# Gated cross-attention and expert layer on one core: the last four second groups of a block are issued between the first groups of the next block

## The reference

```
x = x + tanh(g_xattn) * attention(layernorm(x), ctx, ctx, mask)
t = layernorm(x)                                   # [4096, 128]
gate = softmax(t @ Wg + bg)                        # 8 experts
thr  = sigmoid(t @ Wt + bt) * 0.125
w = max(gate - thr, 0);  w = w / sum(w)
h  = gelu(einsum('td,edf->etf', t, W1) + b1)       # 8 experts x 512
eo = einsum('etf,efd->etd', h, W2) + b2
out = x + tanh(g_ffn) * einsum('te,etd->td', w, eo)
```

## Time and profile before

| what | value |
|---|---|
| median of 3 runs | 737.56 us (735.87 to 740.76) |
| profiled execution, its own time | 733.51 us |
| its span (first to last instruction) | 731.4 us |
| mean granted TensorE clock | 0.975 of full |
| busy: TensorE, VectorE, ScalarE, GpSimd | 89%, 71%, 58%, 25% of the span |

### The profile page before, as it was taken

How to read it: one execution, slowest core, us unless ns; L and a number is a source line. 1 busy time by engine, 2 the same in 40 slices (tenths; PEclk the granted TensorE clock), 3 DMA queues, 4 the chain that set the end, 5 groups by cost and what they waited for, 6 DMA issues and landing times.

```text
span 731.4 us, 14293 instructions
## 1 busy us (share of the span) xinstructions
PE 647.9 (89%) x3944; PEld 482.2 (66%) x3944; DVE 522.8 (71%) x1083; ACT 422.0 (58%) x764; POOL 179.7 (25%) x218
## 2 busy tenths in 40 slices
PE   3679888888899888884799999999999999999996
PEld 2446566556666666542587787877878778787784
DVE  5577676677677766662578687786877868778786
ACT  4225555555555555543575776757766676676673
POOL 6133333322333222321012022121221212202122
PEclk9879999999999999998799999999999999999999
DMA  6333333333333333330311112111111111211120
GB/s 189 109 97 104 103 98 97 91 83 104 94 99 96 92 95 104 103 97 2 49 60 45 57 44 59 53 49 56 44 57 43 57 44 56 57 43 50 40 67 14
DMA packets 48420, 53.09 MB, mean 73 GB/s; under 512 B 9616, under 2 KB 34832, under 8 KB 48400
## 3 DMA queue, kind: packets, MB, share of 16 engines
q1 hardware_dynamic: 48400, 52.85, 26.3%
HBM read 27.01 MB, written 2.23 MB: 40 GB/s over the span
## 4 chain that ended last, share of the span: by engine, by line
PE 65%; DVE 9%; issue 7%; DMA 6%; ACT 5%; SPq 4%; POOL 3%; DVEq 1%; POOLq 0%; ACTq 0%
PE ps_y L1067 8%; PE ps_y L1069 7%; PE ps_y L1068 7%; PE ps_h L1089 7%; PE ps_h L1087 7%; PE ps_h L1088 7%; PE scores L1025 5%; DMA k_masked<-k_stack 5%; PE scores L1026 4%; SPq L396 4%; POOL yT L544 3%; ACT part L577 2%; DVE k_stack L702 2%; PE scores L1017 2%; PE misc L886 2%
## 5 line engine op out<-in xcount | busy, mean ns | idle before, releaser
L650 ACT ACTIVATE h_sb<-ps_h,b_sb 128x512 f32<-128x512 f32 x256 | 175.2, 689 | 116.5 <-PE ps_h L1089 103.2
L857 DVE TENSOR_TENSOR h_low<-h_sb,h_high 128x512 fp32r<-128x512 f32 x256 | 164.5, 683 | 0.0
L544 POOL TENSOR_TENSOR yT<-yT,weighted 128x512 f32<-128x512 f32 x56 | 72.3, 1290 | 309.2 <-DVE weighted L845 308.5
L853 DVE CAST h_high<-h_sb 128x512 fp32r<-128x512 f32 x128 | 87.0, 680 | 81.6 <-ACT h_sb L650 81.6
L679 DVE TENSOR_REDUCE neg_max<-scores 128x4 f32<-128x512 f32 x128 | 86.7, 689 | 70.8 <-PE scores L1026 70.1
L563 ACT ACTIVATE probs<-scores 128x512 f32<-128x512 f32 x128 | 77.1, 604 | 60.0 <-PE scores L1018 60.0
L1067 PE MATMUL ps_y<-h_high,w_high 128*128 128x512 f32 x256 | 102.2, 399 | 5.0 <-DVE h_low L857 5.0
L1087 PE MATMUL ps_h<-x_high,w_high 128*128 (+1 forms) x256 | 101.8, 398 | 0.0
L1069 PE MATMUL ps_y<-h_high,w_low 128*128 128x512 f32 x256 | 101.3, 396 | 0.0
L1089 PE MATMUL ps_h<-x_high,w_low 128*128 (+1 forms) x256 | 101.0, 394 | 0.0
L1068 PE MATMUL ps_y<-h_low,w_high 128*128 128x512 f32 x256 | 100.8, 394 | 0.0
(11 more groups left out here) (122 smaller groups left out, 981.5 us busy)
## 6 DMA issues: line engine op xcount, KB each, us to landing
w_row<-w_scratch SPq DMA_DIRECT2D x64, 256.0 KB, 3.2
k_masked<-k_stack SPq DMA_DIRECT2D x64, 128.0 KB, 2.5
k_cur<-k_stack SPq DMA_DIRECT2D x16, 512.0 KB, 3.0
q_masked<-q_stack SPq DMA_DIRECT2D x64, 96.0 KB
w_raw<-in_w_ffn SPq DMA_DIRECT2D x17, 256.0 KB, 2.7
ctx_sb<-in_ctx SPq DMA_DIRECT2D x17, 128.0 KB, 2.1
out_y<-y_out SPq DMA_DIRECT2D x8, 256.0 KB, 3.4
mask_words<-in_mask SPq DMA_DIRECT2D x17, 32.0 KB, 1.8
```

Of the source, the lines that this page charges most:

```text
L544: nc.gpsimd.tensor_tensor(yT[:], yT[:], weighted[:, e % 2, :], ALU.add).then_inc(added, 1)
L650: nc.scalar.activation(h_sb[:, j % HBUF, :], ps_h[:, j % 4, :], ACT.Gelu_apprx_tanh, bias=b1_sb[:, j:j + 1]).then_inc(h_done, 1)
L853: V.tensor_copy(h_high[:, j % HBUF, :], h_sb[:, j % HBUF, :]).then_inc(high_odd, 1)
L857: V.tensor_tensor(h_low[:, j % HBUF, :], h_sb[:, j % HBUF, :], h_high[:, j % HBUF, :].bitcast(F32), ALU.subtract).then_inc(low2_done, 1)
```

## The change

TensorE: in blocks 1 to 7, s(28) to s(31) of the block before are issued behind h(0) to h(3), in the places where the LAG leaves a gap. Those of the last block follow the loop. The output transposes of the block before move from behind h(2) to behind s(2), which is behind h(6) (j == LAG + 2). s(0) now waits for combine 6 of the block before, no longer for combine 7 (the wait on weighted_done is g * E + (e - 1) for all e).

VectorE: combines 6 and 7 of the block before move to steps 0 and 4 of the next block, behind low(j + 1), and finish(g - 1) from step 2 to step 6. Those of the last block follow the loop.

GpSimd, ScalarE and SyncE have unchanged programs.

```diff
--- before.py
+++ after.py
@@ -861,13 +861,16 @@
                     high(j + 1)
                     low(j)
                     low(j + 1)
-                    if j == 2 and not (isinstance(g, int) and g == 0):
+                    later = not (isinstance(g, int) and g == 0)
+                    if j % FC == 0 and j >= FC + LAG:
+                        combine(g, (j - LAG) // FC - 1)
+                    elif j % FC == 0 and later:
+                        combine(g - 1, (j + CH - LAG) // FC - 1)
+                    if j == LAG + 2 and later:
                         finish(g - 1)
-                    if j >= FC + LAG and j % FC == 0:
-                        combine(g, (j - LAG) // FC - 1)
-                for e in range((CH - LAG) // FC - 1, E):
-                    combine(g, e)
             loop_b(dve, body_b)
+            combine(NB - 1, E - 2)
+            combine(NB - 1, E - 1)
             finish(NB - 1)
 
 
@@ -1059,7 +1062,7 @@
                 e, f = divmod(j, FC)
                 if f == 0:
 
-                    wait_count(pe, weighted_done, g * E + (e - 1) if e >= 2 else g * E)
+                    wait_count(pe, weighted_done, g * E + (e - 1))
                 pe.wait_ge(high_odd if j % 2 else high_even, g * (CH // 2) + (j // 2 + 1))
                 pe.wait_ge(low2_done, g * CH + (j + 1))
                 dst = ps_y[:, e % 2, :]
@@ -1087,13 +1090,16 @@
                     mm(dst, w_high[:, e, cols], xh, start=True, stop=False)
                     mm(dst, w_high[:, e, cols], xl, start=False, stop=False)
                     mm(dst, w_low[:, e, cols], xh, start=False, stop=True).then_inc(h_full, 1)
-                    if j == 2 and not (isinstance(g, int) and g == 0):
-                        untranspose(g - 1)
+                    later = not (isinstance(g, int) and g == 0)
                     if j >= LAG:
                         second(g, j - LAG)
-                for j in range(CH - LAG, CH):
-                    second(g, j)
+                    elif later:
+                        second(g - 1, CH + j - LAG)
+                    if j == LAG + 2 and later:
+                        untranspose(g - 1)
             loop_b(pe, body_b)
+            for j in range(CH - LAG, CH):
+                second(NB - 1, j)
             untranspose(NB - 1)
```

## The result

The changed kernel takes 755.64 us (median; 754.03 to 756.41) against 736.71 before on the same chip: ratio 1.0244, 95% interval 1.0200 to 1.0287. It is **slower**, by 18.9 us. Forecast were 751.2 and a range of 744.3 to 757.5. One execution of e1_t_late, 880.03 us at a mean granted clock of 0.68, was in a slow state and counts in no ratio.

A forecast was written before the change was run, and what follows sets the result against it. TensorE was taken as the bound, with 1.99 us lost at each of seven block seams. Seams +10.9 and clock falls +2.7 on 737.56 gave 751.2 us, range 744.3 to 757.5.

The forecast's parts named there:

- The wait of s(30) goes: At block seams, s(30), a second matmul group, no longer waits for VectorE's h_low; saves 0.68 us and a 0.1 hitch.
- h(0) waits instead, 0.36: At a block's first matmul group, TensorE waits for the gelu of group 31 of the block before; 0.36 us with hitch.
- T waits 2.69: A block's four output transposes, behind s(2), wait 2.69 us for the last add, which follows VectorE's moved combine 7.
- VectorE and GpSimd have room: At seams, the copy beside add 6 adds 0.76 us to VectorE, covered by 0.8 at least; finish costs nothing.
- Transfers hidden: Output store and w_row loads are not delayed; expert 3's load has 16 groups of 1.38 us against 3.2 landing time.
- Seam +1.56: Each of seven block seams costs 3.55 us after against 1.99 before: +1.56, seven times +10.9 us.
- rival D: VectorE falls behind at seams: copy beside add 6 and finish add 0.8 us each, 756.8 us; 5%.
- The clock: TensorE's 2.5 us idle at T lowers the clock in one to two of seven seams, 1.8 us each: +2.7 us.
- Rival A: Every seam loses the clock: +23.5 us, 761.1 us; 5%.
- B: At seams T does not wait, the last add being over when TensorE gets there: 729.7 us, faster; 5%.

The follow-up runs named there:

- e1_t_late: Changed kernel with the output transposes T two slots later (behind s(4), not s(2)) and finish in step 10: 729.06 us, 0.9931 of before.
- e5_h0_wait: Changed kernel with h(0) to h(3) waiting for the gelu of the group four back, not all 32 groups of the block before: 746.17 us, 1.0147 of before.
- e9_filler_h0: Changed kernel with 11 unused matmuls ahead of T's wait and h(0) to h(3) waiting only for the group four back: 745.77 us, 1.0130 of before.
- e4_t_plus1: Changed kernel with T one slot later (behind s(3)) and finish in step 8: 739.45 us, 1.0058 of before.
- e2_combine_early: Changed kernel with only combine 7 moved, from step 4 to step 2 on VectorE; T stays behind s(2): 735.21 us, 0.9997 of before.
- e3_filler: Changed kernel with 11 extra unused matmuls ahead of T's wait in blocks 1 to 7: 749.94 us, 1.0190 of before.

## Why the prediction was right

By its steps:

1. *The wait of s(30) goes.* It did; one h_low wait is left at each end of the stage.
2. *h(0) waits instead, 0.36.* Right in place and cause, and it comes in all seven seams, though the waits list six: in the first seam h(0) is only 0.24 late. The term was too small for the others: 0.44 and a hitch of 0.1, 0.54 (e5_h0_wait and e9_filler_h0: 3.8 to 3.9 us in seven). The hop from ScalarE to TensorE was taken as 0.06 to 0.13 and is 546.19 - 545.95 = 0.24 in this seam.
3. *T waits 2.69.* 2.54 in the first seam, 2.70 in the second, 2.77 to 2.79 in the five others. That combine and T keep the distance they have in the steady order is shown by e4_t_plus1 and e1_t_late from one side and e2_combine_early from the other.
4. *VectorE and GpSimd have room.* Right (rival D didn't come): no new wait on VectorE in the seams. The slow copy beside add 6 mattered only in e2_combine_early, where combine 7 stood behind it.
5. *Transfers hidden.* No wait on a w_row load or on the output store shows in the waits.
6. *Seam +1.56.* Measured +1.82 in a seam without a fall: 0.18 more from h(0) and 0.09 more from T's wait make up the difference. In the profiles the stage grew by 18.6 where 13.6 were forecast: 1.8 of the 5.0 are the seams (less 0.4 in the first), 3.5 the falls (6.2 against 2.7). The first median lay 4.4 above 751.2, the second 0.8.
7. *The clock.* The mechanism is shown by e3_filler, the price of 1.8 was 1.54, the number of one to two was too low: four, four and three in the three profiles with this wait (the changed kernel's two and e5_h0_wait's). After idle times of 2.4 to 2.6 us, as the trace counts them, it fell in 11 of 21 seams, a share that the two rows of before with their opposite answers the earlier trace rows had left open. The row of 727.16 could not settle it: TensorE had only T's 0.66 us of work left behind that wait, and the granted clock did fall at 729.3.

The first median lies outside the 748.5 to 753.9 that the forecast gave its 76%, and inside the range because its top was set for rival D "with up to four falls". The four falls came, D didn't: the sum itself had 2.7 us for the falls, and that the room left for another cause took up the rest is luck.

Rival A (every seam falls) did not come: four, four and three seams of seven fell. B (T doesn't wait) needed another place of combine 7 or of T. e1_t_late comes nearest to it, with 729.1 against the 729.7 that was worked out for B, but the two agree by luck: B's gain was put at 7.9 us from a base of 737.56, and e1_t_late's medians lie 6.2 apart, from a base of 735.25, and its stage 5.4, as h(0) cost more than the 0.36 of the sum.

## What to carry over

When work is moved from the end of one block into the next, look for what waits on that work there: here the transposes moved, the chain in front of them moved further, and a wait of 0.6 became 2.8. The steady state of the same order gives such a distance before anything is run: take when the chain's last link ends and when the waiting engine gets to its place, both counted from the same matmul. Two places for one wait (TensorE's or VectorE's program) are two cures of different worth, and a wait that is in the open may be covering another one, so that removing it in the old order brings nothing.

## What the runs showed of the hardware

Idle time of TensorE of 2.4 to 2.6 us, as the trace counts it, took the clock from 2.4 to 1.2 GHz in 11 of 21 seams, each time for about 3.4 us and at a price of 1.4 to 1.7 us, and with waits of 1.0 to 1.2 us (e4_t_plus1) and 0.5 to 0.8 us (e2_combine_early) in none of 14. The fall can come after the wait, with TensorE at work again (at 560.2, when T had started at 558.76). Eleven matmuls that nobody needs, put into the wait, made the expert stage 5.3 us shorter in the profile.

In the looped blocks h(0) started later behind the gelu that released it. The first seam of the changed kernel is written out:

```profile
401.73 0.69 ACT L650 ACTIVATE h_sb<-ps_h,b_sb 128x512 f32<-128x512 f32 x1
...
402.47 0.50 PE L1090 MATMUL ps_h<-x_high,w_high 128*128 128x512 f32 x1
```

Here h(0) starts 0.05 behind the gelu's end (401.73 + 0.69), as T does behind GpSimd's add (509.41 + 1.26 to 510.72); in the looped blocks it was 0.24 (above), so h(0) is 0.24 late here and 0.44 there. Whether it is the loop that adds the 0.2 wasn't tried; without the wait (e5_h0_wait) h(0) starts in cadence in the looped blocks too.
